# Attention values of two steps multiplied together behind the scores of the even step, and the key turn placed before or behind the key/value product by parity

## The chip, the cores and the metric

The kernel runs on one core of a Trainium2 chip. The metric is the time of one execution on the device in microseconds (us). The kernel before took 1129.91 us in the median of three runs (1127.69 to 1133.77). The granted TensorE clock averaged 0.989 of full speed in the profiled execution.

## The reference

One transformer layer on x (4 batches of 512 rows of 256), with a context of 1024 rows per batch. A gated cross attention (16 heads of 64) is followed by a gated mixture of experts:

```python
lat = layer_norm(_layernorm(x), ln_lat_g, ln_lat_b)
ctx = layer_norm(context, ln_ctx_g, ln_ctx_b)
q = lat @ Wq                                  # 16 heads of 64
k, v = jnp.split(ctx @ Wkv, 2, axis=-1)
k = apply_rope(k, cos, sin)                   # the rotation of the keys
attn = jnp.clip(q @ k.T * 64 ** -0.5, -11.0, 11.0)
out = jnp.einsum('bhns,bhsd->bhnd', softmax(attn), v)
x = x + tanh(g_xattn) * (out @ Wo + bo)
h = gelu(x_n @ w1[e] + b1[e]); y = h @ w2[e] + b2[e]   # x_n = _layernorm(x), e: the best 2 of 4 experts
x = x + tanh(g_ffn) * (gated sum of y over the two experts, corrected by constants)
```

Only the attention is touched by the change.

## The kernel before, in words

**Stages.** From the start of the span to 39 us the first keys and values are made. The attention loop runs from 39 to about 852 us. The experts run from there to the end at 1129.6 us. All matrix products work in fp32 or in split fp32r (a high and a low part, three products).

**The attention loop.** `attention` calls `step(b, u, s, last)` for 4 batches b, 4 units u of four heads, and 8 steps s, on every engine in the same order. Each engine works through its own list strictly in that order, and semaphores join the lists. Inside a batch i = 8u + s counts the steps from 0 to 31. A unit holds two pairs p of heads with four steps c = s % 4 each, and a step takes 256 of the 1024 context rows, as two halves i = 0, 1. So s even means c = 0 or 2, s odd means c = 1 or 3. While a unit is being worked on, the keys and values of the next unit are made, one tile of 128 context rows in each step.

**A step on TensorE**, with a letter for each group of matmuls, by which the prediction speaks of them:
- S: `score` of both halves, into the banks sc0 and sc1 (L1800, 12 matmuls, tile mode 64*128).
- T: `k_turn`, the transposition of the rotated keys that the step before made, into the bank tr (L1786, 2 matmuls, mode 128*128).
- K: `kv_make`, keys and values of the next unit, into the bank kv (L1745 to L1747, 6 matmuls, mode 128*128). In most steps T comes before K. In the steps that the code calls `turned` K comes before T.
- D: `denominators` in c = 0 (L1824, mode 128*32). P: `project` in s = 2 and 3, the output product of the unit before (mode 128*128). Q: `q_make` in c = 1, the queries of the next pair (mode 128*128).
- V: `values` of the step before, prob by val into the bank pv (L1814, 8 products that show as 16 matmuls, mode 128*32). In before it comes in every step, behind all of the above.
- C: `ctx_turn` in i = 18 to 25 of a batch that isn't the last, and `lat_turn` in i = 26 and 27: normalised rows of the next batch transposed into the bank tr (L1752, L1759). C waits for `k_ready` of the same step's T: `k_low` on VectorE must have read tr. These ten steps, with i = 18 to 27, are named turned steps below (the code's own `turned` holds for i = 19 to 28, and for the router's steps 9 and 10). In i = 8 and 9 `x_turn` stands in the same place with the same wait.
- In the last unit of the last batch (`is_direct`) no K or T is left, and `direct` sums the denominators from prob itself in each step.

**A step on ScalarE:** `exps` of both halves (L932, prob from sc), `kv_evac` (L877 k_raw and L878 val, from kv), `k_split` (L870, the high part of the keys from tr), and in turned steps `ctx_affine` or `lat_affine`.

**A step on VectorE:** `normalise` (c = 1) or `q_low` (c = 2) first, then `clamp` of both halves (L1159), `rot_cos` (L1147, reads kv, waits for kv_evac), `k_low` (L1111, reads tr, waits for k_split), `ctx_low` in turned steps (L1097), `sums` of both halves for c above 0 (L1171, L1174), with `residual` between them in s = 2 and 3. Then come `reciprocals` in c = 0, `o_low` in c = 1, and `ctx_stats` and `ctx_norm` of the next batch.

**A step on GpSimd:** `rotate` (L716 with k_raw, then L720 behind rot_cos), in turned steps two small operations for the norm, and in the last batch scatters by indirect DMA.

**Buffers.** prob has two slots, by s % 2. kv, pv, tr and mi are single banks. K waits until rot_cos has read kv, and S waits until the exponentials of the step before have read sc.

Of the kernel before, what the change touches and what calls it, by code (L numbers as in the profile page):

```python
# [32 lines left out]
def flamingo_kernel(nc, x, ctx_in, g_xattn, g_ffn, cos, sin, lat_g, lat_b, ctx_g, ctx_b, w_q, w_kv, w_o, b_o,  # L33
# [9 lines left out]
    UNITS = INNER // (4 * DH)  # L43
# [4 lines left out]
    STEPS = 2 * CH  # L48
# [14 lines left out]
    with ExitStack() as stack:  # L63
# [6 lines left out]
        def sem(name):  # L70
            return stack.enter_context(nc.semaphore(name))
# [196 lines left out]
        pv_done = sem("pv_done")  # L268
# [75 lines left out]
        def step_no(b, u, s):  # L344
            return b * BS + (u * STEPS + s)
# [4 lines left out]
        def kv_no(b, u, t):  # L350
            return b * BS + (u * ST + t)
# [13 lines left out]
        def wait(eng, semaphore, count):  # L365

            if count > 0:
                eng.wait_ge(semaphore, count)

        def k_part(u, t, part):  # L370

            return kst[:, u % 2, :, part, t * P:(t + 1) * P]
# [53 lines left out]
        def is_direct(b, u):  # L426

            return b == B - 1 and u == UNITS - 1
# [36 lines left out]
        def is_first(b, u):  # L465
            return b == 0 and u == 0
# [5 lines left out]
        def next_unit(b, u):  # L472
            return (b, u + 1) if u + 1 < UNITS else (b + 1, 0)
# [386 lines left out]
        def _(act):  # L860
# [5 lines left out]
            def k_split(b, u, t):  # L866

                act.wait_ge(k_tr, kv_no(b, u, t) + 1)

                a.activation(k_part(u, t, 0), tr[:, 0:UW].rearrange("p (j s) -> p j s", j=2), ACT.Copy).then_inc(k_out, 1)  # L870
# [55 lines left out]
            def exps(b, u, s, i):  # L926
                act.wait_ge(sc_ready[i], step_no(b, u, s) + 1)

                c, q = s % CH, pair_no(b, u * 2 + s // CH)
                if not (is_direct(b, u) and s > 1):  # L930
                    wait(act, summed[i], q * 3 - 1 if c == 0 else q * 3 if c == 1 else q * 3 + 1)
                a.activation(prob[:, s % 2, i, :], sc[i][:], ACT.Exp, scale=DH ** -0.5).then_inc(exp_done[i], 1)  # L932

            def x_out(b, hf, bank, raw):
# [49 lines left out]
            def step(b, u, s, last):  # L984
                i = u * STEPS + s
                p, c = u * 2 + s // CH, s % CH
                make = not (last and u == UNITS - 1)
                exps(b, u, s, 0)
                exps(b, u, s, 1)
                if make:  # L990
                    kv_evac(*next_unit(b, u), s)
                if s == 0:
                    k_split(b, u, ST - 1)
                elif make:
                    k_split(*next_unit(b, u), s - 1)
                if c == 1 and not (is_first(b, u) and s == 1):
                    o_round(*((b, p - 1) if p else (b - 1, PAIRS - 1)))
                if s == 3 and make:
                    wq_round(*next_unit(b, u))
                if s == (WO_AT if is_direct(b, u) else STEPS - 1):  # L1000
                    wo_round(b, u)
                if is_first(b, u) and s == 4:
                    act.wait_ge(ld_small, 16 * 5)
                    a.activation(gates2[:, 2:4], gates2[:, 0:2], ACT.Tanh).then_inc(tanh_ready, 1)
                if not last and 0 <= i - TURN < ST:
                    ctx_affine(b + 1, i - TURN, tr)
                if not last and 0 <= i - L_TURN < 2:
                    lat_affine(b + 1, i - L_TURN, tr)
                if c == 1 and not (last and p == PAIRS - 1):
                    q_round(*next_pair(b, p))  # L1010

                if i - X_TURN in (0, 1):
                    x_out(b, i - X_TURN, tr[:], 0)
                if last and i == R_RANK + 1:
                    act.wait_ge(f_diff, 1)
                    a.activation(f_tmp[:, 0:EARLY, :], f_logit[:, 0:EARLY, :], ACT.Exp).then_inc(f_exp, 1)
                if is_direct(b, u):
                    for piece in ROUNDS_AT[s]:
                        piece_round(piece)
                    if s == SLOTS_AT:  # L1020
                        slots_round(0)
# [58 lines left out]
        def _(dve):  # L1080
# [27 lines left out]
            def k_low(b, u, t):  # L1108

                dve.wait_ge(k_out, kv_no(b, u, t) + 1)  # L1110
                v.tensor_tensor(k_part(u, t, 1), tr[:, 0:UW].rearrange("p (j s) -> p j s", j=2),  # L1111
                                k_part(u, t, 0).bitcast(F32), ALU.subtract).then_inc(k_ready, 1)
# [128 lines left out]
            def step(b, u, s, last):  # L1241
# [3 lines left out]
                make = not (last and u == UNITS - 1)  # L1245
# [32 lines left out]
                clamp(b, u, s, 1)  # L1278
                if done_rows and s == STEPS - 2:
                    rows_keep(b - 1)  # L1280
                if make:
                    rot_cos(*next_unit(b, u), s)
                if s == 0:
                    k_low(b, u, ST - 1)
                elif make:
                    k_low(*next_unit(b, u), s - 1)
                if i - X_TURN in (1, 2):
                    logits(b, i - X_TURN - 1)
                if last and i == R_RANK + 2:
# [450 lines left out]
        def _(pe):  # L1740
# [183 lines left out]
            def step(b, u, s, last):  # L1924
                i = u * STEPS + s
                p, c = u * 2 + s // CH, s % CH
                make = not (last and u == UNITS - 1)
                nb, nu = next_unit(b, u)
                score(b, u, s, 0)
                score(b, u, s, 1)  # L1930
                asked = i - X_TURN in (1, 2)
                turned = asked or not last and 0 <= i - TURN - 1 < ST + 2
                if make and turned:
                    kv_make(nb, nu, s)
                if i == X_TURN + 3:
                    pe.wait_ge(f_lout, 2 * b + 3)
                if last and i == R_RANK + 3:
                    pe.wait_ge(r_read, 1)
                if s == 0 or make:

                    if asked:
                        router(b, i - X_TURN - 1, tr, 0, UW // E)
                    elif turned and i - TURN - 1 < ST:
                        pe.wait_ge(c_affd, tile_no(b + 1, i - TURN - 1) + 1)
                    elif turned:
                        pe.wait_ge(l_affd, 2 * (b + 1) + i - L_TURN)
                    k_turn(*((nb, nu, s - 1) if s else (b, u, ST - 1)))
                if make and not turned:
                    kv_make(nb, nu, s)
                if c == 0 and not (is_first(b, u) and s == 0):  # L1950

                    pe.wait_ge(q_ready, pair_no(b, p) + 1)
                    wait(pe, wo_out, (b * UNITS + u) * 2 - (2 if s == 0 else 0))
                    if not (is_direct(b, u) and s == CH):
                        denominators(*((b, p - 1) if p else (b - 1, PAIRS - 1)))
                if s in (2, 3) and not is_first(b, u):

                    pe.wait_ge(q_ready, pair_no(b, p + 1) + 1)
                    wait(pe, wo_out, (b * UNITS + u) * 2 + s - 4)
                    project(*((b, u - 1) if u else (b - 1, UNITS - 1)), s - 2)  # L1960
                if c == 1 and not (last and p == PAIRS - 1):

                    wait(pe, den_turned, pair_no(b, p))
                    q_make(*next_pair(b, p))
                if not (is_first(b, u) and s == 0):
                    values(*((b, u, s - 1) if s else (b, u - 1, STEPS - 1) if u else (b - 1, UNITS - 1, STEPS - 1)))
                if is_direct(b, u) and s:
                    direct(b, u, s - 1)
                if not last and TURN <= i < L_TURN + 2:

                    pe.wait_ge(k_ready, kv_no(nb, nu, s - 1) + 1 if s else kv_no(b, u, ST - 1) + 1)
                    if i < L_TURN:
                        ctx_turn(b + 1, i - TURN, tr)
                    else:
                        lat_turn(b + 1, i - L_TURN, tr)
                if i - X_TURN in (0, 1):

                    pe.wait_ge(k_ready, kv_no(nb, nu, s - 1) + 1 if s else kv_no(b, u, ST - 1) + 1)
                    pe.wait_ge(f_lout, 2 * b + i - X_TURN + 1)
                    pe.wait_ge(f_norm, b * NT + 2 * (i - X_TURN) + 2)  # L1980
                    x_turn(i - X_TURN, tr)
                if last and i == R_RANK + 1:
                    pe.wait_ge(k_ready, kv_no(nb, nu, s - 1) + 1)
                    count_slots()
                if is_direct(b, u) and s == SLOTS_AT:
                    pe.wait_ge(k_ready, B * BS)
                    slots_turn(0)
# [106 lines left out]
```

## Time and profile before

| What | us |
|---|---|
| Median of three runs | 1129.91 |
| The profiled execution | 1131.16 |
| Its span | 1129.6 |
| TensorE busy | 1070.9 (95%) |
| VectorE busy | 948.4 (84%) |
| ScalarE busy | 653.1 (58%) |
| GpSimd busy | 540.6 (48%) |

Busy time of TensorE isn't work at its peak, since matmuls are pipelined. In timelines two neighbouring groups overlap a little for the same reason. The price of a group is therefore best read from its start to the start of the next group. A timeline row has the start, the duration, the engine, the line, the operation, the tiles, the tile mode or shape, the count, and in brackets the idle time before it with what ended it. A row of the windows table has the stretch, its length, the busy time and number of instructions of TensorE, of its weight loads, of VectorE, ScalarE and GpSimd, the granted clock (1.00 is full), the DMA share and GB/s.

### The profile page before, as it was taken

How to read it: one execution, taken by the hardware profiler on the slowest of the kernel's cores; microseconds unless marked ns; L12 is line 12 of the kernel's file. 1: busy time of each engine (PE TensorE's matmuls, PEld its weight loads, DVE VectorE, ACT ScalarE, POOL GpSimd, SP SyncE). 2: the span in 40 equal slices, each digit the busy share in tenths (PEclk: the TensorE clock that was granted, in tenths of full speed). 3: DMA queues.
4: the chain of work that ended last, by engine and by line, in shares of the span. 5: the costliest groups of instructions: out<-in, count | busy, mean ns of one | idle time of the engine just before them, and what ended most of it. 6: DMA issues, size and time to landing. Idle time of an engine off the chain costs nothing.

```text
span 1129.6 us, 22455 instructions
## 1 busy us (share of the span) xinstructions
PE 1070.9 (95%) x7949; PEld 713.9 (63%) x7949; DVE 948.4 (84%) x1772; ACT 653.1 (58%) x1259; POOL 540.6 (48%) x551
## 2 busy tenths in 40 slices
PE   5899999999999999999999999999998998799994
PEld 3556555655555565656555565655447997799994
DVE  7898999898889989898998989889976657577675
ACT  5654557655555765555566655444565764567662
POOL 7433475333427633242654334318832646555661
PEclk9999999999999999999999999999999999999998
DMA  7000010000000000000010000601353334545344
GB/s 208 13 10 11 20 38 20 11 10 11 11 19 25 24 12 10 20 10 20 20 29 10 10 14 7 202 1 54 109 192 121 140 113 132 170 151 170 113 149 142
DMA packets 59188, 72.04 MB, mean 64 GB/s; under 512 B 11579, under 2 KB 52167, under 8 KB 59080
## 3 DMA queue, kind: packets, MB, share of 16 engines
q1 hardware_dynamic: 54840, 61.30, 17.5%
q0 software_dynamic: 3360, 8.53, 2.0%
q8 instruction: 66, 1.08, 0.4%
q10 hardware_dynamic: 880, 0.79, 0.2%
q14 instruction: 42, 0.34, 0.1%
HBM read 54.84 MB, written 16.54 MB: 63 GB/s over the span
## 4 chain that ended last, share of the span: by engine, by line
PE 74%; DVE 13%; issue 5%; ACT 3%; POOL 2%; DMA 1%; SPq 0%; ACTq 0%; DVEq 0%; POOLq 0%
PE pv L1814 16%; PE sc L1800 14%; PE kv L1745 5%; PE kv L1747 5%; PE kv L1746 5%; PE sc L1745 4%; PE sc L1747 4%; PE sc L1746 4%; PE tr L1786 3%; PE mi L1745 2%; DVE acc L1174 2%; PE mi L1746 2%; PE mi L1747 2%; PE mi L1824 2%; DVE prob L1159 2%
## 5 line engine op out<-in xcount | busy, mean ns | idle before, releaser
L932 ACT ACTIVATE prob<-sc 128x1024 f32<-128x1024 f32 x256 | 249.5, 1028 | 200.4 <-PE sc L1800 197.5
L716 POOL TENSOR_TENSOR rot_s<-k_raw,sinb 128x256 f32<-128x256 f32 x128 | 112.7, 880 | 381.1 <-ACT k_raw L877 380.9
L1814 PE MATMUL pv<-prob,val 128*32 128x512 f32 x2048 | 245.5, 597 | 2.3 <-DVE recip L1193 2.3
L1159 DVE TENSOR_SCALAR prob<-prob 128x1024 f32<-128x1024 f32 x256 | 181.6, 722 | 43.9 <-ACT prob L932 42.3
L1800 PE MATMUL sc<-q_hid,w2all 64*128 64x512 f32 x1536 | 213.4, 410 | 1.2 <-DVE w2all L1139 1.2
L1800 PEld LDWEIGHTS sc<-q_hid,w2all 64*128 64x128 f32 x1536 | 135.1, 185 | 101.4 <-issue 55.1
L1174 DVE TENSOR_TENSOR acc<-acc,prob 128x1024 f32<-128x1024 f32 x120 | 177.4, 1499 | 0.0
L720 POOL TENSOR_TENSOR rot_c<-rot_c,rot_s 128x256 f32<-128x256 f32 x128 | 111.6, 872 | 37.6 <-DVE rot_c L1147 23.0
L1814 PEld LDWEIGHTS pv<-prob,val 128*32 128x32 f32 x2048 | 56.5, 109 | 111.2 <-issue 90.4
L1745 PE MATMUL kv<-w2all,acts 128*128 128x512 f32 x248 | 109.8, 443 | 2.2 <-DVE acts L1105 1.3
L1745 PE MATMUL sc<-w2all,q_hid 128*128 x304 | 89.8, 295 | 18.1 <-DVE q_hid L1647 17.4
L1747 PE MATMUL kv<-w2all,acts 128*128 128x512 f32 x248 | 98.5, 397 | 0.0
L1746 PE MATMUL kv<-w2all,acts 128*128 128x512 f32 x248 | 98.0, 395 | 0.0
L1746 PE MATMUL sc<-w2all,q_hid 128*128 x304 | 86.7, 285 | 0.0
L1747 PE MATMUL sc<-w2all,q_hid 128*128 x304 | 86.6, 285 | 0.0
L1171 DVE TENSOR_TENSOR acc<-prob 128x1024 f32<-128x1024 f32 x60 | 85.4, 1461 | 0.0
L877 ACT ACTIVATE k_raw<-kv 128x256 f32<-128x256 f32 x124 | 48.7, 392 | 53.8 <-PE kv L1747 51.4
L1147 DVE TENSOR_TENSOR rot_c<-kv,cosb 128x256 f32<-128x256 f32 x124 | 52.2, 421 | 28.5 <-ACT val L878 22.9
L1745 PEld LDWEIGHTS sc<-w2all,q_hid 128*128 128x128 f32 x304 | 58.7, 193 | 21.4 <-issue 21.2
L779 POOL TENSOR_TENSOR acts<-prob,acts 128x512 fp32r<-128x512 f32 x36 | 48.3, 1343 | 42.8 <-ACT acts L955 41.1
L1030 ACT ACTIVATE sc<-sc,c_aff 128x256 f32<-128x256 f32 x78 | 34.9, 447 | 50.6 <-PE sc L1747 50.1
L1786 PE MATMUL tr<-ident,rot_c 128*128 128x128 f32 x256 | 54.5, 295 | 8.9 <-POOL rot_c L720 8.8
(315 smaller groups left out, 2377.4 us busy)
## 6 DMA issues: line engine op xcount, KB each, us to landing
prob<-in_L_ffn_w SPq DMA_DIRECT2D x17, 1024.0 KB, 5.3
slots_x<-lat_r SPq DMA_DIRECT2D x1, 5016.0 KB, 18.8
rows<-slots_x SPq DMA_DIRECT2D x19, 264.0 KB, 4.4
rows<-in_ctx SPq DMA_DIRECT2D x32, 128.0 KB, 2.2
w_raw<-in_L_xattn_Wq SPq DMA_DIRECT2D x16, 256.0 KB, 2.7
w_raw<-in_L_xattn_Wo SPq DMA_DIRECT2D x64, 64.0 KB
acc<-in_L_ffn_w SPq DMA_DIRECT2D x16, 256.0 KB, 4.0
acc<-in_L_ffn_w SPq DMA_DIRECT2D x5, 512.0 KB
```

The source lines that it names most:

```text
L716: g.tensor_tensor(rot_s[:].rearrange("p (h a c) -> p h a c", h=4, a=2), kh[:, :, ::-1, :], sinb[:, t].unsqueeze(1).to_broadcast([P, 4, 2, ...
L720: g.tensor_tensor(k_rot[:], rot_c[:], rot_s[:], ALU.add).then_inc(rot, 1)
L932: a.activation(prob[:, s % 2, i, :], sc[i][:], ACT.Exp, scale=DH ** -0.5).then_inc(exp_done[i], 1)
L1159: v.tensor_scalar(prob[:, s % 2, i, :], prob[:, s % 2, i, :], EXP_LOW, EXP_HIGH, ALU.max, ALU.min).then_inc(clamped[i], 1)
L1171: v.tensor_tensor(acc[:, i, :], prob[:, 0, i, :], prob[:, 1, i, :], ALU.add).then_inc(summed[i], 1)
L1174: v.tensor_tensor(acc[:, i, :], acc[:, i, :], prob[:, s % 2, i, :], ALU.add).then_inc(summed[i], 1)
L1745: mm(dst, lhs(0), rhs(0), start=start, stop=False, **kw)
L1746: mm(dst, lhs(0), rhs(1), start=False, stop=False, **kw)
L1747: return mm(dst, lhs(1), rhs(0), start=False, stop=stop, **kw)
L1786: last = nc.tensor.transpose(tr[:, j * P:(j + 1) * P], k_rot[:, j * P:(j + 1) * P], ident[:])
L1800: last = mm(sc[i][:, h * N:(h + 1) * N], kst[rows_h, u % 2, j, lk, t * P:(t + 1) * P], q_sp[rows_h, p % 2, lq, :], start=lk + lq == 0, sto ...
L1814: last = mm(pv[g * 32:(g + 1) * 32, :], val[:, u % 2, 2 * c + i, at:at + 32], prob[:, s % 2, i, h * N:(h + 1) * N], start=c == 0 and i == ...
```

## The change

On TensorE values are no longer multiplied in each step. An even step multiplies those of the two steps before it, s-2 and s-1, directly behind its scores. Odd steps multiply none. The last unit of the last batch keeps its place for all steps but its first. The key turn T comes before K in even steps and behind K in odd steps, whether turned or not, and ScalarE and VectorE take `kv_evac`/`k_split` and `rot_cos`/`k_low` in the same order as TensorE does. Since `exps` of an even step writes the slot of prob that the values of s-2 read, it gets a wait for these on ScalarE.

```diff
@@ exps
                 if not (is_direct(b, u) and s > 1):
                     wait(act, summed[i], q * 3 - 1 if c == 0 else q * 3 if c == 1 else q * 3 + 1)
+                if s % 2 == 0:
+                    wait(act, pv_done, step_no(b, u, s) - 1)
                 a.activation(prob[:, s % 2, i, :], sc[i][:], ACT.Exp, scale=DH ** -0.5).then_inc(exp_done[i], 1)
@@ step of ScalarE
                 exps(b, u, s, 0)
                 exps(b, u, s, 1)
-                if make:
+                if make and s % 2:
                     kv_evac(*next_unit(b, u), s)
                 if s == 0:
                     k_split(b, u, ST - 1)
                 elif make:
                     k_split(*next_unit(b, u), s - 1)
+                if make and s % 2 == 0:
+                    kv_evac(*next_unit(b, u), s)
@@ step of VectorE
-                if make:
+                if make and s % 2:
                     rot_cos(*next_unit(b, u), s)
                 if s == 0:
                     k_low(b, u, ST - 1)
                 elif make:
                     k_low(*next_unit(b, u), s - 1)
+                if make and s % 2 == 0:
+                    rot_cos(*next_unit(b, u), s)
@@ step of TensorE
                 score(b, u, s, 1)
                 asked = i - X_TURN in (1, 2)
                 turned = asked or not last and 0 <= i - TURN - 1 < ST + 2
-                if make and turned:
+                if s % 2 == 0 and not (is_direct(b, u) and s):
+                    for back in (2, 1):
+                        if s:
+                            values(b, u, s - back)
+                        elif not is_first(b, u):
+                            values(*((b, u - 1) if u else (b - 1, UNITS - 1)), STEPS - back)
+                if make and s % 2:
                     kv_make(nb, nu, s)
...
                     k_turn(*((nb, nu, s - 1) if s else (b, u, ST - 1)))
-                if make and not turned:
+                if make and s % 2 == 0:
                     kv_make(nb, nu, s)
...
                     q_make(*next_pair(b, p))
-                if not (is_first(b, u) and s == 0):
-                    values(*((b, u, s - 1) if s else (b, u - 1, STEPS - 1) if u else (b - 1, UNITS - 1, STEPS - 1)))
                 if is_direct(b, u) and s:
+                    values(b, u, s - 1)
                     direct(b, u, s - 1)
                 if not last and TURN <= i < L_TURN + 2:
```

## Rows read from the trace of the kernel before

**Rows 1.** The page, its chain that ended last: shares of the span by engine
```profile
PE 74%; DVE 13%; issue 5%; ACT 3%; POOL 2%; DMA 1%; SPq 0%; ACTq 0%; DVEq 0%; POOLq 0%
```
**Rows 2.** Waits of TensorE, 39 to 851 us: us in total, times, longest
```profile
PE tr L1786 <- POOL rot_c L720: 5.7, 9, 1.4
PE pv L1814 <- DVE recip L1193: 2.3, 1, 2.3
PE tr L1752 <- DVE w2all L1111: 1.5, 3, 0.5
```
**Rows 3.** Windows table: the turned steps of the second batch, with most of step 28
```profile
360.50:427.10 66.60, 66.02 (x481) 38.27 (x480) 61.20 (x108) 46.01 (x97) 33.90 (x35) 1.00 0.07 21
```
**Rows 4.** Timeline of TensorE, one plain step: S, T, K, V, next S
```profile
433.68 1.67 PE L1800 MATMUL sc<-q_hid,w2all 64*128 64x512 f32 x12
435.28 0.44 PE L1786 MATMUL tr<-ident,rot_c 128*128 128x128 f32 x2
435.47 0.48 PE L1745 MATMUL kv<-w2all,acts 128*128 128x512 f32 x1
...
437.04 1.93 PE L1814 MATMUL pv<-prob,val 128*32 128x512 f32 x16
438.89 1.65 PE L1800 MATMUL sc<-q_hid,w2all 64*128 64x512 f32 x12
```
**Rows 5.** Timeline of TensorE, last unit: V, then `direct` in its mode, then S
```profile
845.28 1.92 PE L1814 MATMUL pv<-prob,val 128*32 128x512 f32 x16
847.02 1.05 PE L1839 MATMUL mi<-prob,ones 128*32 128x256 f32 x16
847.99 1.67 PE L1800 MATMUL sc<-q_hid,w2all 64*128 64x512 f32 x12
```
**Rows 6.** Timeline of TensorE, turned steps: S of i = 18, 22, 24 and 28
```profile
352.91 1.67 PE L1800 MATMUL sc<-q_hid,w2all 64*128 64x512 f32 x12
...
381.00 1.66 PE L1800 MATMUL sc<-q_hid,w2all 64*128 64x512 f32 x12
382.59 0.50 PE L1745 MATMUL kv<-w2all,acts 128*128 128x512 f32 x1
...
384.09 0.38 PE L1786 MATMUL tr<-ident,rot_c 128*128 128x128 f32 x2
384.40 1.92 PE L1814 MATMUL pv<-prob,val 128*32 128x512 f32 x16
...
392.59 0.44 PE L1752 MATMUL tr<-ident,rows 128*128 128x128 f32 x2 [0.51 <-DVE w2all L1111]
392.96 1.66 PE L1800 MATMUL sc<-q_hid,w2all 64*128 64x512 f32 x12
...
420.99 1.65 PE L1800 MATMUL sc<-q_hid,w2all 64*128 64x512 f32 x12
```
**Rows 7.** Timeline of VectorE: reciprocals in i = 20, then a stretch of i = 22
```profile
372.72 0.44 DVE L1179 STREAM_TRANSPOSE recip<-mi 128x256 f32<-128x256 f32 x1
...
374.70 0.38 DVE L1085 BATCH_NORM_STATS2 c_bn<-rows 128x6 f32<-128x256 f32 x1
...
385.58 0.42 DVE L1147 TENSOR_TENSOR rot_c<-kv,cosb 128x256 f32<-128x256 f32 x1
...
386.58 2.89 DVE L1174 TENSOR_TENSOR acc<-acc,prob 128x1024 f32<-128x1024 f32 x2
389.39 0.41 DVE L1085 BATCH_NORM_STATS2 c_bn<-rows 128x6 f32<-128x256 f32 x1
...
390.04 0.68 DVE L1159 TENSOR_SCALAR prob<-prob 128x1024 f32<-128x1024 f32 x1
```
**Rows 8.** Timeline of VectorE, plain steps: rot_cos behind K, and a pair of clamps
```profile
437.91 0.42 DVE L1147 TENSOR_TENSOR rot_c<-kv,cosb 128x256 f32<-128x256 f32 x1 [0.23 <-ACT val L878]
...
441.76 1.28 DVE L1159 TENSOR_SCALAR prob<-prob 128x1024 f32<-128x1024 f32 x2
```
**Rows 9.** Windows table, columns as in Rows 3: behind idle time and small matmuls
```profile
736.60:739.00 2.40, 2.40 (x14) 1.50 (x12) 0.00 (x0) 1.02 (x1) 0.00 (x0) 0.61 0.00 0
```

## The prediction

> **What bounds the kernel now.** I first read the chain that ended last by engine: 74% of the span lies on TensorE and 13% on VectorE [rows 1]. The waits of TensorE within the attention loop, read next, show how little is left to win there by removing waits: 5.7 us for the rotated keys (T), 2.3 us for one normalisation in the last unit, 1.5 us of C for `k_low` [rows 2]. The other waits of the loop add up to under 3 us, in 812 us. So the attention is a row of matmuls behind one another. The reader should next see in the windows table that VectorE has no air in the turned steps: 61.2 of 66.6 us busy [rows 3]. A change of order there can cost nothing on TensorE and still lose, if it makes VectorE wait in one place and TensorE in another. Last come the timelines, for the price of each group and the order of the waits.
>
> **Prices of the groups, from start to start.** A plain step costs S 1.60, T 0.19, K 1.57, V 1.85, together 5.21 us [rows 4]. In a turned step S is 1.59, K 1.50, T 0.31 before V, and C 0.37 before S [rows 6]. V is 1.74 when work of its own tile mode follows, `direct` 0.97 before S [rows 5]. So a change of tile mode costs some 0.1 us: 1.85 - 1.74 = 0.11 for V to S, 0.31 - 0.19 = 0.12 for T to V.
>
> **Part 1: plain pairs of steps.** Before, a pair has V twice and six changes of mode. After, the even step is S 1.60, V 1.74, V 1.85, T 0.19, K 1.57 and the odd one S 1.59, K 1.50, T 0.31: 10.35 us, against 10.42. T directly before S stands in no row. Its bounds are 0.19 (no change of mode) and 0.37 (C before S), and I take 0.31, the same group before V, to which it is nearest; that leaves the pair between -0.19 and -0.01 us. Where the even step has D (c = 0), D and V no longer share a mode side by side, so one change of mode comes back: about +0.05 instead. Over a unit that is zero within 0.2 us. The work per se is unchanged.
>
> The Trainium skill (TensorEngine Tiling (Array Packing), Key Properties) says that a change of tiling mode, and not just of tile, drains the engine; the trace agrees, with 0.11 and 0.12 us. Counted group by group, the change removes 58 such changes in the whole loop, most of them in the turned steps (11 in each of three batches). By the rule alone the kernel would be faster; that is rival A.
>
> **Part 2: the wait added to `exps`.** In even steps ScalarE now waits for V(s-2), 1.60 + 1.74 us behind the start of S instead of about 0.8. Behind it in ScalarE's list stand the second exponential, `k_split` and `kv_evac`, and VectorE's clamps wait for it. None of these ends late in plain steps. T and K end 1.60 + 1.74 + 1.85 + 0.19 + 1.57 = 6.95 us behind S, while both exponentials are over by 3.34 + 2 x 1.03 = 5.4 (1.03 us is the page's mean of one). The next S needs them no earlier. V(s-1) needs clamps of the odd step only. What VectorE does lose is time: it idles until the clamps, and again until `rot_cos`, which comes 0.87 us behind K (437.04 to 437.91) [rows 4, 8]. From `rot_cos` of an even step VectorE has, in the heaviest plain pair, two `rot_cos`, two `k_low` (four at 0.34), two pairs of sums of 2.81 and two pairs of clamps of 1.28: 9.5 us of work in a period of 10.35 [rows 7, 8]. Fits, with 0.8 us to spare. Cost: nothing. If that cover is gone, each pair pays what is over.
>
> **Part 3: C loses its cover in odd turned steps.** This is where I expect the time. C must wait until `k_low` has read T out of tr. Before, V (1.85 us) stood between T and C, and still C waited at times, 0.51 us in i = 23 [rows 6]. After, an even step has K between them, but an odd step has S, K, T, then C, with P or Q between only for c = 1 or s = 3. And `k_low` of an odd step stands on VectorE behind the sums of the even step, which stand behind `rot_cos` of the even step, which needs K of the even step. That closes a loop that both engines pass one after the other. For the pair i = 22, 23, from `k_low` landed to `k_low` landed:
> - TensorE: C 0.31 (0.37 at most), S 1.60, V 1.74, V 1.85, T 0.19, K 1.50 = 7.2, with 0.1 for the hand-over 7.3; then 0.87 until `rot_cos` starts: 8.2 us [rows 4 to 6, 8].
> - VectorE: `rot_cos` and `ctx_low` 0.67 (a third each of the 1.00 from 385.58 to 386.58), sums 2.81, statistics and norm 0.65, clamps 1.28, `rot_cos` 0.34, `k_low` 0.41: 6.2 us [rows 7, 8].
>
> Together 14.3 us, where the pair takes 11.96 now (381.00 to 392.96) [rows 6] and TensorE alone would need 10.8. It stands idle for 3.5 us ahead of C. The other pairs go the same way:
> - i = 20, 21: reciprocals 1.98 and a normalisation 0.6 in place of the sums: 14.1. i = 24, 25: the same less the statistics: 13.8.
> - i = 18, 19: no loop yet; 6.9 + 0.87 until `rot_cos`, then 0.34, sums 2.81, `residual` 0.66, statistics, norm and the norm of the latents 0.98, clamps 1.28, `rot_cos` and `k_low` 0.75: 14.6. i = 26, 27: loop with `residual`, no statistics, 0.3 for the longer `lat_turn` and its activations: 14.6.
>
> With 0.55 for the last `lat_turn` the ten steps take 14.6 + 14.1 + 14.3 + 13.8 + 14.6 + 0.55 = 71.95 us. Now they take 420.99 - 352.91 = 68.08 [rows 6]. That is +3.9 us for each of three batches, **+11.6 us**. A bound from below: without the loop TensorE would save 3 changes of mode in most pairs, but VectorE's own work (61.2 us in 66.6) keeps the gain to some 2.3 us per batch, -7 in all. A bound from above: the period of 14.3 in all five pairs with 1 us more for slower VectorE operations, +8 per batch, +24.
>
> **Part 4: small gains.** T in even steps gets 3.6 us of V as cover, in odd ones 1.5 us of K. The 5.7 us of waits for the rotation [rows 2] could go. But 4.6 us of them lie behind 752 us, in the last batch, where VectorE also computes the routing and is without a gap; what T gives back there, the clamps take. I count 1.0 us. `x_turn` in i = 8 and 9 saves two or three changes of mode in four batches, 1 us; Q stands between T and it in i = 9, so that I see no wait. Queues passed: SP and GpSimd change nothing in their lists, and GpSimd's scatters lie ahead of a rotation that now has more time in odd steps and, in even ones, 3.1 us from K to T, of which it uses about 2.3.
>
> **Sum.** 1131.16 (the profiled execution) + 11.6 - 1.0 - 1.0 + 0 = 1140.8. The median lies 1.25 us below the profiled execution, so 1139.5; I take **1139 us**, +0.8%.
>
> **Rivals.**
> - A, faster: the loop of part 3 doesn't bind, because sums, clamps and ScalarE run more side by side than I laid out, and the changes of mode decide: 58 x 0.12 = -7 us with -1 from part 4: 1122 us. For it speaks that mode costs are on the path that TensorE sets; against it, that VectorE has 5.4 us free in 66.6 [rows 3] and that its order is fixed. It decides from the point where `k_low` in i = 23 lands before T ends.
> - B, no change to be measured: the loop binds only in the pair 22, 23 (+2.3 x 3), the lighter pairs win 0.3 each, and part 4 gives 2 to 4 us: 1126 to 1134, say 1131.
> - C, slower by far: idle stretches of 3.5 us let TensorE's clock fall. In the row behind the routing counts it stands at 0.61, so between 2.4 and 1.2 GHz [rows 9]; before it the engine had idled 0.5 us and done 2.6 us of small matmuls. Against it: 2.3 us of idle time in the last unit left it at full. Some 4 us at half speed cost 2 us: +6 for one fall per batch, +18 for three. Or plain pairs overrun their 0.8 us on VectorE by 0.2 each, +9. Either way about 1149, up to 1157. The Trainium skill (TensorE: Matmul & The Clock Gate, HAM oscillation) warns that waits between bursts can throttle the engine again and again; here that is the higher end of C.
> - The change doing other than it says: no; both V's are in TensorE's list by the diff.
>
> **Chances.** Forecast (1134 to 1146) 0.57, A 0.13, B 0.15, C 0.15. The range leaves out most of A and the top of C: **1126 to 1150**. A measurement of this kernel tells about 0.5% (5.7 us) from no change, so the borders are 1124.3 and 1135.6. Faster is A with its lower half of B: 0.13. Same is the rest of B and the lowest part of the forecast: 0.19. Slower is the rest, 0.68.
>
> **What the profile would show.** Right: C in i = 19, 21, 23, 25, 27 waits for VectorE's L1111, about 3.5 us in 23 and 0.5 to 1 us in the others; S of 18 to S of 28 takes 72 us; VectorE waits ahead of L1147 in even steps (1 us and more) and ahead of the first clamp; plain pairs without D, P and Q stay at 10.35; V's two groups run 3.6 us without a gap. Wrong: idle time of TensorE spread over plain steps (C), a turned pair under 11.5 us (A), or a wait that I don't have, for instance S for the exponentials of an even step or K for `rot_cos`.

## The result and the profile after

The changed kernel took 1150.11 us in the median (1148.52 to 1151.64), the kernel before 1130.99 us beside it. The ratio is 1.017, with a 95% interval of 1.0138 to 1.0202. The change makes the kernel slower by 19 us. The prediction said 1139 us in a range of 1126 to 1150. The direction and the place were right. The size was half of what came, and the time lies just above the range. The profiled execution took 1150.31 us.

The page of the changed kernel, its busy times and its chain by engine (the latter answers to [rows 1]):

```profile
span 1148.7 us, 22461 instructions
PE 1073.1 (93%) x7949; PEld 718.1 (63%) x7949; DVE 944.7 (82%) x1772; ACT 663.0 (58%) x1259; POOL 565.3 (49%) x551
...
PE 71%; DVE 14%; issue 6%; POOL 3%; ACT 3%; DMA 1%; SPq 0%; DVEq 0%; ACTq 0%; POOLq 0%
```

The span grew by 19.1 us, the busy time of TensorE by 2.2. So about nine tenths of the loss is idle time of TensorE. The rest is work at a lower clock, less what fewer changes of tile mode save.

The waits of TensorE in the changed kernel's attention loop, 39 to 872 us (total, times, longest). They answer to [rows 2], where C waited 1.5 us in all:

```profile
PE tr L1758 <- DVE w2all L1115: 18.2, 12, 3.8
PE pv L1820 <- DVE recip L1197: 2.7, 2, 2.3
PE tr L1792 <- POOL rot_c L720: 2.5, 2, 1.7
PE kv L1751 <- DVE rot_c L1151: 1.7, 1, 1.7
PE tr L1765 <- DVE w2all L1115: 1.3, 3, 0.4
```

L1758 and L1765 are C, L1115 is `k_low`. These 15 waits are i = 19, 21, 23, 25 and 27 of three batches: 19.5 us in all, 18.0 more than before, where the span grew by 19.1. No other wait is longer than 2.5 us in total except one that stood there before.

The timeline of TensorE in the changed kernel, a plain pair of steps without D, P and Q. It answers to [rows 4]:

```profile
447.12 1.67 PE L1806 MATMUL sc<-q_hid,w2all 64*128 64x512 f32 x12
448.72 3.64 PE L1820 MATMUL pv<-prob,val 128*32 128x512 f32 x32
452.30 0.44 PE L1792 MATMUL tr<-ident,rot_c 128*128 128x128 f32 x2
452.49 0.48 PE L1751 MATMUL kv<-w2all,acts 128*128 128x512 f32 x1
...
454.06 1.66 PE L1806 MATMUL sc<-q_hid,w2all 64*128 64x512 f32 x12
455.65 0.50 PE L1751 MATMUL kv<-w2all,acts 128*128 128x512 f32 x1
...
457.15 0.42 PE L1792 MATMUL tr<-ident,rot_c 128*128 128x128 f32 x2
457.50 1.64 PE L1806 MATMUL sc<-q_hid,w2all 64*128 64x512 f32 x12
```

The reader should see no bracket: nothing waits. The pair takes 10.38 us (447.12 to 457.50), against 10.42 before and 10.35 forecast. T directly before S, which no row of before showed, takes 0.35.

The same engine in the turned steps i = 22, 23 and the start of 24. It answers to [rows 6]:

```profile
396.32 0.38 PE L1758 MATMUL tr<-ident,rows 128*128 128x128 f32 x2
396.63 1.66 PE L1806 MATMUL sc<-q_hid,w2all 64*128 64x512 f32 x12
...
399.72 0.40 PE L1792 MATMUL tr<-ident,rot_c 128*128 128x128 f32 x2
403.95 0.44 PE L1758 MATMUL tr<-ident,rows 128*128 128x128 f32 x2 [3.83 <-DVE w2all L1115]
404.32 2.29 PE L1806 MATMUL sc<-q_hid,w2all 64*128 64x512 f32 x12
406.54 4.60 PE L1820 MATMUL pv<-prob,val 128*32 128x512 f32 x32
411.07 0.44 PE L1792 MATMUL tr<-ident,rot_c 128*128 128x128 f32 x2
```

Two things stand here. C of the odd step waits 3.83 us. Behind that, S takes 2.22 us instead of 1.59 and the two V 4.53 instead of 3.58. The windows table of the changed kernel (columns as in [rows 3]) gives the reason, the granted clock of 0.65 (full is 2.4 GHz and the lower level 1.2 GHz, so this stretch has parts of both):

```profile
399.90:403.90 4.00, 0.23 (x2) 0.00 (x0) 4.00 (x9) 2.90 (x6) 2.48 (x3) 1.00 0.00 0
403.90:408.00 4.10, 4.05 (x22) 1.94 (x26) 3.35 (x4) 1.50 (x4) 2.22 (x3) 0.65 0.01 4
```

While TensorE idles, VectorE is busy for all of the 4.00 us. Its timeline in the same steps (answers to [rows 7, 8]), and one row of GpSimd's:

```profile
397.28 0.42 DVE L1151 TENSOR_TENSOR rot_c<-kv,cosb 128x256 f32<-128x256 f32 x1 [1.13 <-ACT val L878]
...
397.95 2.89 DVE L1178 TENSOR_TENSOR acc<-acc,prob 128x1024 f32<-128x1024 f32 x2
...
401.42 0.68 DVE L1163 TENSOR_SCALAR prob<-prob 128x1024 f32<-128x1024 f32 x1
...
402.11 1.12 DVE L1163 TENSOR_SCALAR prob<-prob 128x1024 f32<-128x1024 f32 x1
403.16 0.41 DVE L1151 TENSOR_TENSOR rot_c<-kv,cosb 128x256 f32<-128x256 f32 x1
403.49 0.41 DVE L1115 TENSOR_TENSOR w2all<-tr,w2all 128x256 fp32r<-128x256 f32 x1
```

```profile
401.81 0.87 POOL L716 TENSOR_TENSOR rot_s<-k_raw,sinb 128x256 f32<-128x256 f32 x1 [0.56 <-ACT k_raw L877]
```

This is the chain of part 3: `rot_cos` of the even step, sums, clamps, `rot_cos` of the odd step, `k_low`. Ahead of it VectorE stands idle for 1.13 us, since K of the even step comes so late.

In the first and third batch the clock was low already when C started, 0.69 us instead of 0.44 (timeline of TensorE in the first batch):

```profile
191.98 0.69 PE L1758 MATMUL tr<-ident,rows 128*128 128x128 f32 x2 [3.82 <-DVE w2all L1115]
192.60 2.93 PE L1806 MATMUL sc<-q_hid,w2all 64*128 64x512 f32 x12
```

From start of S to start of S (before / after), in the second batch:

| Steps | before | after | difference |
|---|---|---|---|
| i = 18, 19 | 14.60 | 15.56 | +0.96 |
| i = 20, 21 | 13.49 | 14.11 | +0.62 |
| i = 22, 23 | 11.96 | 14.83 | +2.87 |
| i = 24, 25 | 13.51 | 15.40 | +1.89 |
| i = 26, 27 | 14.52 | 14.70 | +0.18 |
| ten turned steps, three batches | | | 7.1 + 6.5 + 7.2 = +20.8 |
| everything else in the loop | | | -1.1 |

### The profile page after: what moved, and what is told of

Same layout as the page of the kernel before. It is cut to its first block, busy times and chain, and to the rows that moved or that the text cites. A ratio compares the mean times of both kernels' runs of the same rounds, so it can differ in the third digit from the quotient of the medians.

```text
span 1148.7 us, 22461 instructions
## 1 busy us (share of the span) xinstructions
PE 1073.1 (93%) x7949; PEld 718.1 (63%) x7949; DVE 944.7 (82%) x1772; ACT 663.0 (58%) x1259; POOL 565.3 (49%) x551
## 3 DMA queue, kind: packets, MB, share of 16 engines
q8 instruction: 66, 1.08, 0.4%
## 4 chain that ended last, share of the span: by engine, by line
PE 71%; DVE 14%; issue 6%; POOL 3%; ACT 3%; DMA 1%; SPq 0%; DVEq 0%; ACTq 0%; POOLq 0%
PE pv L1820 17%; PE sc L1806 13%; PE kv L1751 5%; PE kv L1753 4%; PE kv L1752 4%; PE sc L1751 4%; PE sc L1753 4%; PE sc L1752 4%; DVE acc L1178 3%; PE tr L1792 3%; DVE prob L1163 2%; PE mi L1751 2%; PE mi L1753 2%; PE mi L1752 2%; PE mi L1830 2%
## 5 line engine op out<-in xcount | busy, mean ns | idle before, releaser
L716 POOL TENSOR_TENSOR rot_s<-k_raw,sinb 128x256 f32<-128x256 f32 x128 | 117.5, 918 | 360.0 <-ACT k_raw L877 359.9
L1820 PE MATMUL pv<-prob,val 128*32 128x512 f32 x2048 | 236.2, 600 | 2.7 <-DVE recip L1197 2.7
L1163 DVE TENSOR_SCALAR prob<-prob 128x1024 f32<-128x1024 f32 x256 | 186.2, 744 | 51.2 <-ACT prob L934 49.7
L1806 PE MATMUL sc<-q_hid,w2all 64*128 64x512 f32 x1536 | 216.0, 414 | 1.2 <-DVE w2all L1143 1.2
L1178 DVE TENSOR_TENSOR acc<-acc,prob 128x1024 f32<-128x1024 f32 x120 | 171.5, 1450 | 0.0
L720 POOL TENSOR_TENSOR rot_c<-rot_c,rot_s 128x256 f32<-128x256 f32 x128 | 144.2, 1126 | 53.5 <-DVE rot_c L1151 40.2
L1820 PEld LDWEIGHTS pv<-prob,val 128*32 128x32 f32 x2048 | 59.8, 110 | 142.2 <-issue 135.3
L1751 PE MATMUL sc<-w2all,q_hid 128*128 x304 | 89.8, 296 | 17.8 <-DVE q_hid L1653 14.1
L1792 PEld LDWEIGHTS tr<-ident,rot_c 128*128 128x128 f32 x256 | 29.8, 144 | 65.9 <-issue 41.7
L1751 PEld LDWEIGHTS kv<-w2all,acts 128*128 128x128 f32 x248 | 47.3, 191 | 32.3 <-issue 23.9
```

What stands on the lines that cost most here:

```text
L716: g.tensor_tensor(rot_s[:].rearrange("p (h a c) -> p h a c", h=4, a=2), kh[:, :, ::-1, :], sinb[:, t].unsqueeze(1).to_broadcast([P, 4, 2, ...
L720: g.tensor_tensor(k_rot[:], rot_c[:], rot_s[:], ALU.add).then_inc(rot, 1)
L1163: v.tensor_scalar(prob[:, s % 2, i, :], prob[:, s % 2, i, :], EXP_LOW, EXP_HIGH, ALU.max, ALU.min).then_inc(clamped[i], 1)
L1178: v.tensor_tensor(acc[:, i, :], acc[:, i, :], prob[:, s % 2, i, :], ALU.add).then_inc(summed[i], 1)
L1751: mm(dst, lhs(0), rhs(0), start=start, stop=False, **kw)
L1792: last = nc.tensor.transpose(tr[:, j * P:(j + 1) * P], k_rot[:, j * P:(j + 1) * P], ident[:])
```

## The experiments

Theory L: C has lost V as its cover, and closes a loop through both engines. Theory W: it is the added wait of the exponentials on ScalarE that costs. Theory F: the idle stretch of i = 23 lets the clock fall, which costs on its own. The pairs below are read from S to S, as in the table; "the pair 22" is i = 22, 23.

### Values back ahead of C

```diff
+        def odd_turn(b, i):
+            return b < B - 1 and i % 2 == 1 and TURN <= i < L_TURN + 2
...
-                    for back in (2, 1):
+                    for back in (1,) if odd_turn(b, i - 1) else (2, 1):
...
+                if odd_turn(b, i):
+                    values(b, u, s - 1)
                 if not last and TURN <= i < L_TURN + 2:
```

> The changed kernel, but in the five odd turned steps of a batch (i = 19 to 27) the values of the even step before are multiplied ahead of C again, and the next even step multiplies only those of the odd step. Theory L (C has lost its cover and closes a loop through the sums and k_low of VectorE): V between T and C both covers the wait and shortens the TensorE half of the loop by 1.9 us, so the pair i = 22, 23 falls from 14.8 to 13.1 us, the idle time ahead of C in i = 23 from 3.8 to about 2.0, the clock stays full, and the kernel takes about 1133 us. Theory W (the wait of the exponentials for the values on ScalarE is what costs): the wait is gone in these steps too, so also about 1133. This run only shows that the time sits in these steps; if both are wrong it stays at 1150.

Measured: 1137.4 us, with the kernel before at 1134.0 beside it; the ratio is 1.0026 (1.0003 to 1.0050). So nearly all of the loss sits in these five odd steps. The pair 22 takes 13.12 us, as forecast. The clock didn't stay full: it was 0.64 from 398.0 to 400.9 us. The timeline of TensorE in this kernel:

```profile
398.05 0.44 PE L1762 MATMUL tr<-ident,rows 128*128 128x128 f32 x2 [1.97 <-DVE w2all L1119]
398.42 2.60 PE L1810 MATMUL sc<-q_hid,w2all 64*128 64x512 f32 x12
400.96 2.53 PE L1824 MATMUL pv<-prob,val 128*32 128x512 f32 x16
403.42 0.44 PE L1796 MATMUL tr<-ident,rot_c 128*128 128x128 f32 x2
```

So it fell behind an idle time of 1.97 us. S takes 2.54 and V 2.46 us, which is 1.6 us too much; in the other two batches it is about the same (pair 24: 14.85 to 15.20 us).

### The same values, but behind C

The edit is the same but for the place: the call of `values` stands behind the block of C.

> As the run before, but with the values of the even step behind C instead of ahead of it. The exponentials of the next even step wait for nothing then, as in the run before. Theory L: the length of the loop is the same as in the changed kernel (k_low, C, V, S, V, T, K, rot_cos), the idle time ahead of C in i = 23 stays near 3.8 us and the kernel near 1150. Theory W: what the wait of ScalarE cost is gone, about 1133 us as in the run before.

Measured: 1156.4 us against 1134.0, ratio 1.0193 (1.0154 to 1.0232). The waits for `k_low` are the same as in the changed kernel, though no exponential of these steps waits for values of two steps before. First its total, then the timeline of i = 23:

```profile
PE tr L1762 <- DVE w2all L1119: 18.2, 12, 3.8
```

```profile
398.54 0.42 PE L1796 MATMUL tr<-ident,rot_c 128*128 128x128 f32 x2
402.78 0.69 PE L1762 MATMUL tr<-ident,rows 128*128 128x128 f32 x2 [3.82 <-DVE w2all L1119]
403.39 3.11 PE L1824 MATMUL pv<-prob,val 128*32 128x512 f32 x16
406.44 1.66 PE L1810 MATMUL sc<-q_hid,w2all 64*128 64x512 f32 x12
```

Theory W falls. The two kernels differ in which side of C the V stands, and that makes 19 us. Here the fallen clock hits V (3.05 instead of 1.85 us). The profiled execution was the fastest of the five, 1151.2 us at a mean granted clock of 0.985; the others took 1156.1 to 1157.7 at 0.978 to 0.980. So more work ran at the lower clock in them, which is likely some 5 of the 19 us; no trace of them shows it.

### C moved behind the next scores, alone and with the values

In the second kernel of this section the edit of the first experiment is added.

```diff
+                if odd_turn(b, i - 1):
+                    back_u, back_s = divmod(i - 1, STEPS)
+                    pe.wait_ge(k_ready, kv_no(*next_unit(b, back_u), back_s - 1) + 1)
+                    (ctx_turn or lat_turn of step i - 1)
...
-                if not last and TURN <= i < L_TURN + 2:
+                if not last and TURN <= i < L_TURN + 2 and i % 2 == 0:
```

> The changed kernel with one edit: C of an odd turned step moves behind the scores of the next even step. Waits of ScalarE stay. Theory L: S (1.6 us) leaves the loop and covers C, the pair i = 22, 23 takes 13.2 us instead of 14.8, with about 2 us idle ahead of C and the clock full; the other pairs are bound by TensorE: about 1130 us. Theory W: no change, 1150 us.

Measured: 1134.7 us against 1134.0, ratio 1.0003 (0.9985 to 1.0021). The wait of ScalarE is still there and the loss is gone. C of i = 23 waits 1.39 us, and the clock holds (1.00 up to 400 us). The pairs 22 and 24 together take 26.72 us, where C of i = 23 now falls into the second, against 30.23 in the changed kernel and 25.47 before.

> Both edits together: in odd turned steps the values of the even step stand at the end, and C stands behind the scores of the next even step. Theory L: the loop is 4.8 us on TensorE and 6.6 on VectorE, 11.5 us for the pair i = 22, 23, less than or equal to the 11.96 of the kernel before, and the pairs save changes of tile mode: about 1128 to 1130 us. Theory W: about 1133 us, as in the first run.

Measured: 1133.4 us against 1134.0, ratio 0.9992 (0.9974 to 1.0010). The pair 22 takes 12.61 us and not 11.5: C of the even step (i = 22) now waits 1.35 us for `k_low`. From S of i = 18 to S of the next batch it is 92.24 us, against 91.19 before, so the turned steps still lose 1 us per batch. This is the best arrangement that I found with values in pairs, and it can't be told from the kernel before.

### Work taken out of the loop

```diff
+                    w = 64 if b < B - 1 and u * STEPS + s == 22 else 2 * N
-                    v.tensor_tensor(acc[:, i, :], acc[:, i, :], prob[:, s % 2, i, :], ALU.add)
+                    v.tensor_tensor(acc[:, i, 0:w], acc[:, i, 0:w], prob[:, s % 2, i, 0:w], ALU.add)
```

> The changed kernel with the two sums of step i = 22 (three batches) taken over 64 columns instead of 1024; the denominators are wrong for that. It takes 2.6 us off VectorE between rot_cos of the even step and k_low of the odd one, and nothing off TensorE. Theory L: the idle time ahead of C in i = 23 falls from 3.8 to about 1.2 us, the clock doesn't fall behind it, each of three batches gains 2.6 + 1.6 us: about 1137.5 us. Theory W: VectorE only waits longer for the exponentials, 1150 us.

Measured: 1145.8 us against 1132.6, ratio 1.0118 (1.0096 to 1.0141). It gains, but only a part. The pair 22 falls to 13.81 us (14.08 in the third batch), not to 12.2, and C still waits 2.80 us in each batch. Against the expectation the clock fell behind it in two of the three: the pair 24 takes 13.80, 15.42 and 16.42 us. VectorE's timeline of this kernel shows what is late in place of the sums:

```profile
392.78 0.90 DVE L1179 TENSOR_TENSOR acc<-acc,prob 128x64 f32<-128x64 f32 x2
...
395.48 0.69 DVE L1163 TENSOR_SCALAR prob<-prob 128x1024 f32<-128x1024 f32 x1 [1.15 <-ACT prob L934]
```

The clamps now wait for the exponentials. These stand behind the activations of C on ScalarE, which wait for `ctx_low`. A second road through the loop runs beside the sums, only 1.0 us shorter. Two kernels tested that, the exponentials of i = 23 shortened in the same way, alone and with the sums:

> The changed kernel with the two exponentials of step i = 23 (three batches) taken over 64 columns instead of 1024; the attention is wrong for that. ScalarE's road in the loop (ctx_low, activations of C, exponentials, clamps) becomes 1.6 us shorter, VectorE's (sums, statistics, norm, clamps) stays. If VectorE's road is the longer one, the pair i = 22, 23 stays at 14.8 us, with 3.8 us idle ahead of C.

> The changed kernel with both: the sums of i = 22 and the exponentials of i = 23 over 64 columns (denominators and attention are wrong for that). Light sums alone brought the pair i = 22, 23 from 14.8 to 13.8 us and not to 12.2. If that is because ScalarE's road was only 1.0 us shorter, taking both off brings the pair to 12.7 to 12.9 us and the idle time ahead of C to about 1.7. If light sums alone were all that the loop gives, it stays at 13.8.

Measured, one execution each: 1150.1 and 1141.5 us, with the kernel before at 1131.4. With light exponentials alone the pair 22 stays at 14.9 us (14.89 to 15.14). With both it falls to 13.28 in all three batches, below the 13.81 of light sums alone, though not to 12.8. The sums over 64 columns still take 0.82 us, from 2.82, so 2.0 us left the road and not the 2.6 that I expected; and the first clamp still waits 0.35 us for the exponentials. 14.83 - 2.0 + 0.35 is 13.2. So there are two roads, VectorE's is the longer one, and taking 2.0 us of work from it gives 1.0 alone and 1.55 with the other road shortened too.

### TensorE kept busy in its wait

```diff
+                if not last and i == 23:
+                    pe.wait_ge(q_ready, pair_no(b, p + 1) + 1)
+                    for _ in range(14):
+                        mm(mi[:], wkv[:, 0, 0, 0:P], wkv[:, 0, 0, 0:N], start=True, stop=True)
```

> The changed kernel with 14 matmuls of 512 columns into the free bank mi (nothing reads them) between T and C of step i = 23, in the 3.8 us in which TensorE is idle. Theory F (the idle stretch lets the clock fall, which then costs 1.6 to 2.0 us in the scores and values of i = 24): C starts where it did, the granted clock behind it stays 1.00, S takes 1.6 instead of 2.2 and the two V 3.6 instead of 4.5 us; the kernel takes about 1145 us. If the slow scores and values come from something else (bank conflicts with C or the activations), nothing changes: 1150.

Measured: 1146.1 us against 1132.6, ratio 1.0124 (1.0100 to 1.0149). With 14 matmuls more than the changed kernel in each of three steps it is about 5 us faster, by the two ratios (5.8 by the spans of the profiled executions). The timeline of TensorE in this kernel:

```profile
397.66 3.45 PE L1983 MATMUL mi<-w2all 128*128 128x512 f32 x14
401.74 0.44 PE L1758 MATMUL tr<-ident,rows 128*128 128x128 f32 x2 [0.62 <-DVE w2all L1115]
402.10 1.67 PE L1806 MATMUL sc<-q_hid,w2all 64*128 64x512 f32 x12
403.70 3.64 PE L1820 MATMUL pv<-prob,val 128*32 128x512 f32 x32
```

S takes 1.60 and the two V 3.58 us, at a granted clock of 1.00. The pair 22 takes 14.85, 14.84 and 14.85 us, where the changed kernel has 15.08, 14.83 and 15.08: it saves the slow C of two batches. The pair 24 takes 13.80, 13.82 and 13.80 us, where the changed kernel has 15.76, 15.40 and 15.79. The difference, 1.96 + 1.58 + 1.99 = 5.5 us, and 0.5 us in the pair 22, 6.0 in all, is what the fallen clock costs. Theory F holds.

### The two halves of the change

The order of T and K alone, on the kernel before (the edits of the change to `kv_make`, `kv_evac` and `rot_cos`, without those to `values` and `exps`):

> The kernel before with only the second half of the change: T ahead of K in even steps, behind K in odd ones, on all three engines, while values stay in every step at its end. Theory L: V still covers C, so nothing but the fractions of a us of tile modes and a short wait of T for the activations of C in even turned steps: 1131 to 1133 us. If the order of T and K is what costs, it would show near 1150.

Measured: 1136.0 us against 1132.6, ratio 1.0027 (1.0015 to 1.0040). That is 3.4 us longer, a little more than the fractions of a us that I expected, and far from 1150. The pair 22 stays at 11.95 us; from S of i = 18 to S of the next batch it is 92.07 us against 91.19, 0.9 more per batch, with T waiting 0.3 us in i = 24 and 0.4 in i = 28 for the activations of C.

Values in pairs alone (the order of T and K as before, so `make and turned` and `make and not turned` again):

> The changed kernel with the order of T and K of the kernel before: values in pairs, but T ahead of K in all plain steps and behind it in the turned ones. In a plain odd step only S (1.6 us) then lies between K of the even step and T, which needs the rotated keys 2.3 us behind K: some 0.7 us idle in each of about 45 plain odd steps. In even turned steps C comes right behind T and has no cover either. Expected 1175 to 1195 us. If the order were only a matter of tile modes, it would stay at 1150.

Measured: 1168.0 us against 1132.6, ratio 1.0305 (1.0277 to 1.0332). That is less than I expected. T waits for the rotated keys in 19 places and not in 45, for instance here (timeline of this kernel, a pair without D, P and Q):

```profile
56.10 1.65 PE L1802 MATMUL sc<-q_hid,w2all 64*128 64x512 f32 x12
58.34 0.44 PE L1788 MATMUL tr<-ident,rot_c 128*128 128x128 f32 x2 [0.58 <-POOL rot_c L720]
```

I had overlooked D and P, which stand between K of the even step and the next S in three of four pairs and hide the rotation there. The other half came as expected: C waits 20.8 us in 24 places, even steps among them, where it stands right behind T; in the changed kernel it is 18.2 us in 12. So the order by parity belongs to the pairs of values: without it they cost 35 us instead of 19.

## Why the prediction was wrong

- **The bound and the prices (parts 1 and 2): right.** Plain pairs: 10.35 forecast, 10.38 measured; with D +0.05 forecast and +0.05 measured (12.64 to 12.69). The added wait costs nothing in plain steps. VectorE's 0.8 us of spare time sufficed.
- **The loop (part 3): right in mechanism, place and order of size.** Forecast waits: about 3.5 us in i = 23 and 0.5 to 1 in the others. Measured in the second batch: 1.38, 0.57, 3.83, 0.30, 0.43. From C to C the pair 20 takes 14.1 us (375.0 to 389.1), as forecast. Moving C, or V ahead of it, takes the loss away, and moving V behind it doesn't.
- **A term of it was too small: the clamps.** I took 1.28 us from a plain step. In i = 23 the two take 1.74 (401.42 to 403.16), because the second runs beside GpSimd's L716 and takes 1.12. The same holds in i = 19 (1.14). The kernel before had the slow clamp in the same two steps, so that its own trace could have given the term. Timeline of VectorE in before, i = 23; the fast one ahead of it stands in [rows 7]:

```profile
390.74 1.13 DVE L1159 TENSOR_SCALAR prob<-prob 128x1024 f32<-128x1024 f32 x1
```

  The pair 22 takes 14.83 us (second batch) instead of 14.3. The pair 18 was forecast up to C, which starts 15.2 us behind S instead of 14.6. With the clock kept full (TensorE kept busy) the ten steps take 73.0 us, against 71.95 forecast: 1.1 us per batch, 3.2 in all. The two slow clamps make up about 1.0 of each 1.1. The Trainium skill (SBUF — State Buffer, Who interferes with whom) says that VectorE, in some of its operations, and GpSimd contend for a shared pair of ports, and that whichever starts first holds it for its whole instruction. The trace agrees: of the single clamps in the changed kernel's loop, all 17 that take 1.08 us or more start while a GpSimd product of 128x256 or 128x512 runs, and end 0.54 to 0.57 us behind it; 26 others run beside L716 but start before it, or at most 0.03 us behind its start, and take 0.7. No run here took L716 away.
- **The step that failed: the clock, which I had as rival C and not in the sum.** I argued from the 2.3 us of idle time in the last unit that left the clock full. Behind 3.8 us of idle time it fell in all three batches, and cost 1.6 to 2.2 us each, 6.0 in all. The price (2 us for a fall) was right. The chance was not: a wait of 3.5 us that I forecast myself on the engine should have carried the fall with it. The Trainium skill (TensorE: Matmul & The Clock Gate, HAM oscillation) says that waits between bursts of matmuls can throttle the engine; here the trace agrees, with the granted clock of 0.65 behind the wait.
- **The sum.** 11.6 forecast for the turned steps; with 3.2 for the clamps and 6.0 for the clock 20.8, and 20.8 measured. The pair 24 shows both halves: 13.8 us forecast, 13.80 measured with the clock kept full, 15.4 to 15.8 with the fall.
- **Part 4** named 2 us, and outside the turned steps the spans differ by 1.7 (20.8 - 19.1), but its parts came out otherwise. The pair of `x_turn` saves 0.18 us in three batches, and in the first `x_turn` waits 0.98 us for `k_low`, in i = 8, a wait that I hadn't seen. In the last batch i = 10 to 19 gain 3.3 us. Of that 2.1 lie in i = 12 and 13, where the clock stays full behind the routing counts (S takes 1.65 us from 757.88; before it took 2.55 from 736.65, at the 0.61 of [rows 9]). The last unit gives 3.0 back; 1.8 of that is no loss, since the values of i = 22 are now multiplied in i = 24 and were in i = 23 before.
- **Rivals.** A fell: the changes of tile mode save what the rows say (-0.04 in a plain pair), but the loop binds. B fell, as the loop binds in all five pairs. The half of C about VectorE's spare time fell too; its half about the clock came true. In the chances, faster counts a lower half of B, though all of B (from 1126) lies above the border of 1124.3; the 0.13 is A's alone.

For a fall in every batch rival C named +6, or 1145 us in all (its "either way about 1149" fits only its other half), and I let the range end at 1150 without adding its other terms. With the clock in the sum and the clamps taken from a turned step, the same working gives 1131.2 + 20.8 - 2.0 - 1.25 = 1148.7 us. The 1.25 us for the median was not borne out either: of four executions of the kernel before, the median was 1130.99, only 0.2 below the profiled one.

## What to carry to other kernels

When work moves between two groups of matmuls, ask what it covered where it stood: a wait that was never seen may have been hidden by it. Then follow each wait that loses its cover around, through all queues, until it comes back to where it began; its length is the new period. A wait of 2 to 4 us on TensorE can cost more than its own length, as here the matmuls behind it ran at the lower clock in most cases: price the two together. And take the duration of an operation from the step in question, not from a plain one.

## What the runs showed of the hardware

- The length of an idle stretch alone doesn't tell whether the clock falls. Behind the same 2.80 us, in the same place of three batches (light sums), it fell in two and stayed full in one. It fell behind 1.97 us (values ahead of C), and not behind 2.31 us in the last unit of the kernel before [rows 2], where what comes before and behind differs. What decides I didn't isolate.
- One fall cost 1.6 to 2.2 us in the changed kernel, with S and two V behind it, and 2.9 in the third batch of light sums (0.27 in the pair 22, 2.62 in the pair 24); matmuls whose result nobody reads prevented it and paid for themselves by 5 us.
- A fp32 `tensor_scalar` of 128x1024 on VectorE takes 0.69 us, also beside GpSimd's product of 128x256 where it starts first. Where that product is running already it takes 1.08 to 1.23 us, and ends some 0.55 us behind it.
